# Proj matmuls two steps behind, staging five steps earlier, and the epilogue in one piece, in a fused attention and FFN kernel on eight cores

## The chip, the cores and the metric

The kernel runs on the 8 NeuronCores of one Trainium2 chip. The time is the device time of the slowest core in microseconds (us), the median of the runs given.

## The reference

The input x is 16 x 2048 tokens of 1024 features, in fp32. The reference is one pre-norm layer:

```python
x = x + attn(layernorm(x))
x = x + ffn(layernorm(x))
# attn: softmax(logits, axis=1), over a single head: every weight is 1,
#   so values are the sum of v over the sequence, times w_o: one row per batch
# ffn:
h = einsum('btd,hd->bth', x, absmean(W_fc))        # 1024 -> 4096, weights -1, 0, 1
h = gelu(h)
h = layernorm(h, ln_w, ln_b)                       # over the 4096
out = einsum('bth,dh->btd', h, absmean(W_proj))    # 4096 -> 1024, weights -1, 0, 1
```

`absmean` rounds each weight, divided by the mean of their absolute values, to -1, 0 or 1.

## The kernel before

Each core has two batches, 4096 tokens. A first stage of about 637 us reads x and the weights, works out the attention's row for each batch (ATT), and leaves the ternary weights in SBUF as bf16: `qf` for fc and `qp` for proj. The rest, the main stage, goes over 16 tiles of 256 tokens (two groups tg of 128), with 32 steps j in each, one per 128 hidden features. Activations in fp32 are split into three bf16 parts that add up to them, so each product is done three times.

Every engine has its own program in order, and the order is written out by hand; semaphores with constant counts tie them together. A step j of tile i is:

- TensorE, fc(j): 24 matmuls (3 parts x 8 slices of 128 input features) into `fc_ps[j % 2]`. It waits until gelu(j-2) has read that buffer (`ss_gelu`).
- ScalarE: gelu(j) from `fc_ps` into the single buffer `g`, after gps(j-1) is done with it (`sv_gdone`), and its square into `gsq`.
- VectorE, "gps(j)" in this text: it adds `g` to S1 and `gsq` to S2 (the sums for the layernorm; at j = 0 two copies), and splits `g` times ln_w into the three parts of a `gps` buffer, four operations; six in all. It waits with the first part until proj(j-2) has read the buffer (`st_projj`), and then counts `sv_gdone` up.
- TensorE, proj(j-1), right after fc(j): 12 matmuls into `proj_ps`, which gathers over the 32 steps. Proj 0 also waits for `sv_psr`, that is, until both halves of `proj_ps` of the tile before are evacuated.

Beside this, work for the tile i+1 is placed in the steps of tile i. VectorE does it after gps(j): x1 = x + ATT into one of four `x1s` buffers (`emit_x1_add`; it waits for the load of x, and with `sm_outs` for the store that was the last to read the buffer), its mean and variance (`emit_x1_bn`), the normalisation into `xs` (`emit_apply`), and 16 blocks that split `xs` into bf16 parts `l2t` (`emit_stage_block`, four operations each). TensorE transposes them into `trp_ps` (`emit_group_T`, 48 in all, two per step from j = 12; each waits for its block, `sv_stg`, and for ScalarE's evacuation of the one two before), and ScalarE copies them back to `l2t` (`emit_group_evac`). ScalarE also takes the square roots for the variances, for which it changes its activation table and changes it back.

At the end of a tile ("the boundary") TensorE does proj 31 and the transposes that are left. VectorE splits S1 and S2, TensorE sums them across partitions by four "S transposes" (L749), ScalarE evacuates these, VectorE makes mean and variance, and ScalarE two roots ("the roots", `ss_r3`). The epilogue of tile i-1 then lies in steps 0 to 5 of tile i, a piece after each gps: evacuation of `proj_ps[0]`, scaled and added to x1s; the same for `proj_ps[1]`; then for each group an operation with U and an addition of V, after which (`sv_y3`) POOL stores the group. Tile 15 has its epilogue in one piece at the end (`emit_epilogue`).

Of the kernel before, what the change touches and what calls it, by code (L numbers as in the profile page):

```python
# [64 lines left out]
def build_nc(nt=NTILE, do_b=True, do_main=True):  # L65
# [18 lines left out]
    with es:  # L84
# [27 lines left out]
        gps_t = sb("gps_t", (128, 1536), BF16)  # L112
        gps = [[gps_t[:, (k * 3 + s) * 256:(k * 3 + s) * 256 + 256] for s in range(3)]
               for k in range(2)]
# [101 lines left out]
        def emit_proj(tensor, i, jj):  # L216
            cglob = 32 * i + jj
            tensor.wait_ge(sv_gdone, cglob + 1)
            if jj == 0:
                if i >= 1:  # L220
                    tensor.wait_ge(sv_psr, 2 * i)
                else:
                    tensor.wait_ge(B_qp, 32)
                    tensor.wait_ge(B_uvbc, 2)
            last = None
            for tg in range(2):
                for s in range(3):
                    for hh in range(2):
                        last = tensor.matmul(out=proj_ps[tg][:, 512 * hh:512 * hh + 512],  # L229
                                      lhsT=gps[jj % 2][s][:, 128 * tg:128 * tg + 128],  # L230
                                      rhs=qp[jj][:, 512 * hh:512 * hh + 512],
                                      start=(jj == 0 and s == 0),
                                      stop=(jj == 31 and s == 2),
                                      skip_group_check=True)
            last.then_inc(st_projj, 1)

        def emit_epi_piece(vector, ii, piece):
            tg = piece // 3 if piece >= 2 else piece
            gr0, gr1 = 2 * ii, 2 * ii + 1
            if piece == 0:  # L240
                vector.wait_ge(ss_r3, ii + 1)
                vector.wait_ge(st_projj, 32 * (ii + 1))
                for tg_ in range(2):
                    vector.tensor_scalar(out=nmrc[tg_][:], in0=m3c[tg_][:],
                                         scalar1=r3c[tg_][:], scalar2=-2.0,
                                         op0=OP.mult, op1=OP.mult)
                vector.scalar_tensor_tensor(out=x1s[gr0 % 4][:], in0=proj_ps[0][:],
                                            scalar=r3c[0][:], in1=x1s[gr0 % 4][:],
                                            op0=OP.mult, op1=OP.add)
                vector.inc(sv_psr, 1)  # L250
            elif piece == 1:
                vector.scalar_tensor_tensor(out=x1s[gr1 % 4][:], in0=proj_ps[1][:],
                                            scalar=r3c[1][:], in1=x1s[gr1 % 4][:],
                                            op0=OP.mult, op1=OP.add)
                vector.inc(sv_psr, 1)
            elif piece in (2, 4):
                tg_ = 0 if piece == 2 else 1
                gr = 2 * ii + tg_
                vector.scalar_tensor_tensor(out=x1s[gr % 4][:], in0=U[:],
                                            scalar=nmrc[tg_][:], in1=x1s[gr % 4][:],  # L260
                                            op0=OP.mult, op1=OP.add)
            else:
                tg_ = 0 if piece == 3 else 1
                gr = 2 * ii + tg_
                vector.tensor_add(out=x1s[gr % 4][:], in0=x1s[gr % 4][:], in1=V[:])
                vector.inc(sv_y3, 1)
# [21 lines left out]
        def emit_x1_add(vector, ip1, tg):  # L288
            gr = 2 * ip1 + tg
            vector.wait_ge(sm_xs[gr % 2], 16 * (gr // 2 + 1))  # L290
            if gr >= 4:
                vector.wait_ge(sm_outs[gr % 4], 16 * (gr // 4))
            vector.tensor_add(out=x1s[gr % 4][:], in0=xs[gr % 2][:],
                              in1=ATT[gr // 16][:])

        def emit_x1_bn(vector, ip1, tg):
            gr = 2 * ip1 + tg
            vector.bn_stats(out=bnp[:, 0:6], in_=x1s[gr % 4][:, 0:512])
            vector.bn_stats(out=bnp[:, 6:12], in_=x1s[gr % 4][:, 512:1024])
            vector.bn_aggr(out=bno2[:, 2 * tg:2 * tg + 2], in_=bnp[:])  # L300
            vector.tensor_scalar_add(out=varc[:], in0=bno2[:, 2 * tg + 1:2 * tg + 2],
                                     scalar1=EPS)
            vector.reciprocal(out=rcc[tg][:], in_=varc[:])
            vector.inc(sv_stat, 1)

        def emit_x1_stats(vector, ip1, only_tg=None):
            for tg in ((0, 1) if only_tg is None else (only_tg,)):
                emit_x1_add(vector, ip1, tg)
                emit_x1_bn(vector, ip1, tg)
# [114 lines left out]
        def _(scalar):  # L424
# [72 lines left out]
            for i in range((nt + 1) if do_main else 0):  # L497
# [14 lines left out]
                if i <= nt - 1:  # L512
                    if i == 0:
                        for q in range(48):
                            emit_group_evac(scalar, 0, q)
                    scalar.preload_act_table(AF.Gelu)
                    for j in range(32):
                        cglob = 32 * i + j
                        scalar.wait_ge(st_fcj, cglob + 1)
                        if cglob >= 1:  # L520
                            scalar.wait_ge(sv_gdone, cglob)
                        scalar.activation(out=g[j % 2][:], in_=fc_ps[j % 2][:],
                                          func=AF.Gelu)
                        scalar.inc(ss_gelu, 1)
                        scalar.activation(out=gsq[j % 2][:], in_=g[j % 2][:], func=AF.Square)
                        scalar.inc(ss_gsq, 1)
                        if j in (8, 10) and i + 1 <= nt - 1:
                            tg = 0 if j == 8 else 1
                            scalar.preload_act_table(AF.Sqrt)
                            scalar.wait_ge(sv_stat, 2 * (i + 1) + tg + 1)  # L530
                            scalar.activation(out=r2c[tg][:], in_=rcc[tg][:],
                                              func=AF.Sqrt)
                            scalar.inc(ss_r2, 1)
                            scalar.preload_act_table(AF.Gelu)
                        if i + 1 <= nt - 1 and 13 <= j <= 31:
                            emit_group_evac(scalar, i + 1, 2 * (j - 13))
                            emit_group_evac(scalar, i + 1, 2 * (j - 13) + 1)
                    if i + 1 <= nt - 1:
                        for q in range(38, 48):
                            emit_group_evac(scalar, i + 1, q)  # L540
                    scalar.preload_act_table(AF.Sqrt)

        @block.tensor
        def _(tensor):
# [163 lines left out]
            for i in range(nt):  # L708
# [3 lines left out]
                for j in range(32):  # L712
# [16 lines left out]
                    if j >= 1:  # L729
                        emit_proj(tensor, i, j - 1)  # L730
                    if i + 1 <= nt - 1 and 12 <= j <= 31:
                        emit_group_T(tensor, i + 1, 2 * (j - 12))
                        emit_group_T(tensor, i + 1, 2 * (j - 12) + 1)
                emit_proj(tensor, i, 31)
                if i + 1 <= nt - 1:
                    for ql in range(40, 48):
# [18 lines left out]
        def _(vector):  # L755
# [160 lines left out]
            for i in range(nt):  # L916
                for j in range(32):
# [11 lines left out]
                    if cglob >= 2:  # L929
                        vector.wait_ge(st_projj, cglob - 1)  # L930
                    vector.tensor_scalar_mul(out=gps[j % 2][0][:], in0=g[j % 2][:],
# [3 lines left out]
                                                in1=gps[j % 2][0][:],  # L935
                                                op0=OP.mult, op1=OP.subtract)
                    vector.tensor_copy(out=gps[j % 2][1][:], in_=rrq1[:])
                    vector.tensor_tensor(out=gps[j % 2][2][:], in0=rrq1[:],
                                         in1=gps[j % 2][1][:], op=OP.subtract)
# [70 lines left out]
```

## Time and profile before

| | |
|---|---|
| median of 3 runs | 3812.06 us (3811.46 to 3812.66) |
| profiled execution, its own time | 3809.74 us |
| span of its slowest core, first to last instruction | 3808.2 us |
| spans of the eight cores | 3804.8 to 3808.2 us |
| mean granted TensorE clock, each core | 0.956 of full speed |
| TensorE busy | 2973.5 us |
| VectorE busy | 2238.7 us |
| ScalarE busy | 908.2 us |

The profile is one execution, seen on core 3, the slowest. Times in it are microseconds from the start of the span. PE is TensorE, DVE is VectorE, ACT is ScalarE; PEclk is the share of its full clock that TensorE was granted. Nearly all operations of VectorE and ScalarE go through one helper and carry its line, L51, so that they are told apart by the tiles that they write and read. Idle time of an engine that isn't the bottleneck costs nothing.

### The profile page before, as it was taken

The page shows a single profiled execution, that of the slowest core. Times are in us where ns is not written, and L with a number is a line of the kernel's source. Part 1 is how long each engine was busy: PE and PEld are TensorE (multiplying, and loading weights), DVE is VectorE, ACT ScalarE, POOL GpSimd, SP SyncE. Part 2 cuts the span into 40 slices and gives each one's busy share as a digit, 9 for nine tenths or more (in the row PEclk, how much of TensorE's full clock was granted, in tenths as well). Part 3 has the DMA queues.
Part 4 walks back from the last instruction along what each step waited for, and adds up shares of the span by engine and source line. Part 5 has one row for each costly group of instructions (what it writes and reads, how often), then busy time and mean ns, then how long its engine had stood idle before and what let it go on. Part 6 is the DMA issues. An engine that isn't in the chain of part 4 may idle for free.

```text
span 3808.2 us, 66893 instructions; the slowest of 8 cores (3804.8 to 3808.2 us)
## 1 busy us (share of the span) xinstructions
PE 2973.5 (78%) x22170; PEld 1989.3 (52%) x22170; DVE 2238.7 (59%) x5462; ACT 908.2 (24%) x2163; POOL 71.5 (2%) x148
## 2 busy tenths in 40 slices
PE   0002334989898998989898989898989898989896
PEld 0002232656565665656565656565656565656564
DVE  5667774656565555556555555555556565656554
ACT  1125202222222222222222222222222222222211
POOL 0000202000000000000000000000000000000000
PEclk9999999999999999999999999999999999999998
DMA  4439450000000000000000000000000000000000
GB/s 144 126 117 287 147 155 23 7 7 12 12 12 12 12 12 12 12 12 12 12 12 12 12 12 7 18 7 18 7 18 7 12 12 12 12 7 12 1 12 12
DMA packets 38403, 130.26 MB, mean 34 GB/s; under 512 B 7216, under 2 KB 7344, under 8 KB 38064
## 3 DMA queue, kind: packets, MB, share of 16 engines
q1 hardware_dynamic: 18864, 67.22, 5.9%
q10 hardware_dynamic: 9216, 33.56, 2.8%
q0 software_dynamic: 9984, 25.20, 1.9%
q8 instruction: 184, 3.01, 0.3%
q14 instruction: 155, 1.27, 0.1%
HBM read 109.15 MB, written 16.78 MB: 33 GB/s over the span
## 4 chain that ended last, share of the span: by engine, by line
PE 69%; DVE 12%; ACT 4%; DMA 4%; DVEq 4%; issue 4%; ACTq 1%; POOL 1%; SPq 0%; POOLq 0%
PE fc_ps L723 34%; PE proj_ps L229 33%; DVEq L50 4%; DVE cols L51 3%; DMA x1s<-wpT 2%; DVE gps_t L51 2%; DMA xs<-wfcT 1%; DVE rrq L51 1%; PE trp_ps L704 1%; DVE bnp L51 1%; ACTq L50 1%; ACT ATT L51 1%; DVE l2t_t L51 1%; DVE x1s L51 1%; ACT g L51 1%
## 5 line engine op out<-in xcount | busy, mean ns | idle before, releaser
L229 PE MATMUL proj_ps<-qp_t,gps_t 128*128 128x512 bf16 x6144 | 1442.3, 385 | 155.6 <-DVE x1s L51 139.1
L723 PE MATMUL fc_ps<-l2t_t,qf_t 128*128 128x256 bf16 x12288 | 1495.2, 281 | 0.7 <-ACT l2t_t L51 0.7
L723 PEld LDWEIGHTS fc_ps<-l2t_t,qf_t 128*128 128x128 bf16 x12288 | 1224.3, 101 | 211.5 <-issue 1.6
L229 PEld LDWEIGHTS proj_ps<-qp_t,gps_t 128*128 128x128 bf16 x6144 | 607.7, 99 | 803.0 <-issue 205.2
L51 DVE TENSOR_TENSOR S<-S,g 128x256 f32<-128x256 f32 x496 | 211.0, 425 | 859.9 <-ACT g L51 855.2
L51 ACT ACTIVATE g<-fc_ps 128x256 f32<-128x256 f32 x512 | 197.1, 385 | 2136.8 <-PE fc_ps L723 2095.8
L51 DVE SCALAR_TENSOR_TENSOR rrq<-g,lnw_c,gps_t 128x256 f32<-128x256 f32 x512 | 248.3, 485 | 41.0 <-issue 3.3
L51 ACT ACTIVATE l2t_t<-trp_ps 128x128 bf16<-128x128 f32 x768 | 213.2, 278 | 135.3 <-PE trp_ps L704 74.0
L51 DVE TENSOR_TENSOR gps_t<-rrq,gps_t 128x256 bf16<-128x256 f32 x512 | 217.6, 425 | 39.9 <-issue 2.6
L51 DVE TENSOR_TENSOR S<-S,gsq 128x256 f32<-128x256 f32 x496 | 210.9, 425 | 37.8 <-issue 1.5
L51 ACT ACTIVATE gsq<-g 128x256 f32<-128x256 f32 x512 | 213.3, 417 | 42.4 <-issue 1.4
L704 PE MATMUL trp_ps<-identb,l2t_t 128*128 128x128 bf16 x768 | 123.5, 221 | 118.8 <-DVE l2t_t L51 92.9
L557 PE MATMUL trp_ps<-identb,l2t_t 128*128 128x128 bf16 x48 | 6.6, 299 | 265.9 <-DVE l2t_t L51 264.7
L51 DVE TENSOR_SCALAR gps_t<-g,lnw_c 128x256 bf16<-128x256 f32 x512 | 180.8, 353 | 41.4 <-issue 1.7
L704 PEld LDWEIGHTS trp_ps<-identb,l2t_t 128*128 128x128 bf16 x768 | 75.1, 98 | 220.8 <-issue 149.5
L51 DVE CAST gps_t<-rrq 128x256 bf16<-128x256 f32 x512 | 150.6, 294 | 40.5 <-issue 3.4
L557 PEld LDWEIGHTS trp_ps<-identb,l2t_t 128*128 128x128 bf16 x48 | 4.0, 123 | 268.2 <-issue 267.6
L51 ACT ACTIVATE cols<-cols 128x1 f32<-128x1 f32 x96 | 22.4, 233 | 283.5 <-DVE cols L51 280.4
L51 DVE TENSOR_TENSOR l2t_t<-rrq,l2t_t 128x128 bf16<-128x128 f32 x256 | 74.7, 292 | 21.7 <-issue 3.2
L51 DVE TENSOR_TENSOR rrq<-xs,l2t_t 128x128 f32<-128x128 f32 x256 | 74.8, 292 | 19.1
L407 POOL DMA_DIRECT2D out<-x1s x32 | 17.1, 533 | 3177.6 <-DVE x1s L51 3177.6
L51 DVE CAST l2t_t<-xs 128x128 bf16<-128x128 f32 x256 | 58.2, 227 | 23.7 <-issue 0.5
(127 smaller groups left out, 1412.8 us busy)
## 6 DMA issues: line engine op xcount, KB each, us to landing
x1s<-wpT ACTq DMA_DIRECT2D x64, 512.0 KB, 4.9
xs<-x SPq DMA_DIRECT2D x64, 512.0 KB, 4.2
xs<-wfcT SPq DMA_DIRECT2D x64, 512.0 KB, 4.5
out<-x1s POOLq DMA_DIRECT2D x32, 512.0 KB, 3.0
x1s<-wvT POOLq DMA_DIRECT2D x8, 512.0 KB, 7.0
x1s<-woT POOLq DMA_DIRECT2D x8, 512.0 KB, 6.6
l2t_t<-gps_t POOLq DMA_DIRECT2D x96, 0.2 KB, 1.6
xs<-ident SPq DMA_DIRECT2D x1, 64.0 KB, 9.1
```

What stands on the lines that cost most here:

```text
L50: self._eng.drain()
L51: ins = attr(*a, **kw)
L229: last = tensor.matmul(out=proj_ps[tg][:, 512 * hh:512 * hh + 512], lhsT=gps[jj % 2][s][:, 128 * tg:128 * tg + 128], rhs=qp[jj][:, 512 * h ...
L407: gpsimd.dma_start(out=og[gr, :, :], in_=x1s[gr % 4][:]).then_inc(sm_outs[gr % 4], 16)
L557: last = tensor.matmul(out=trp_ps[g_ % 2][:], lhsT=lhs, rhs=identb[:], start=(s_ == 0), stop=(s_ == 2), skip_group_check=True)
L704: tensor.matmul(out=trp_ps[ql % 2][:], lhsT=lhs, rhs=identb[:], start=True, stop=True, skip_group_check=True).then_inc(st_tr, 1)
L723: last = tensor.matmul(out=fc_ps[j % 2][:], lhsT=qf[d][:, 128 * j:128 * j + 128], rhs=l2t[i % 2][s][d][:], start=(s == 0 and d == 0), stop ...
```

## The change

- `gps` has three buffers in place of two, and gps(j) waits for the third proj before it in place of the second. TensorE does proj(j-2) after fc(j) in place of proj(j-1); proj 30 and 31 follow after the last step.
- The epilogue of tile i-1 stands in one piece ahead of gps(0) of tile i.
- The statistics of tile i+1 are done at j = 0 (first group) and j = 2, in one piece each, in place of j = 6 to 9; the applies at j = 5 and 6 in place of 10 and 11; the blocks at j = 7 to 22 in place of 12 to 27.
- ScalarE takes both roots for them at j = 4, with one change of table and back, in place of j = 8 and 10 with one each. Transposes start at j = 10 in place of 12 and their evacuations at 11 in place of 13; after the last step 4 and 6 of them are left in place of 8 and 10.

```diff
-        gps_t = sb("gps_t", (128, 1536), BF16)
+        gps_t = sb("gps_t", (128, 2304), BF16)
...
-               for k in range(2)]
+               for k in range(3)]
...
-                                      lhsT=gps[jj % 2][s][:, 128 * tg:128 * tg + 128],
+                                      lhsT=gps[cglob % 3][s][:, 128 * tg:128 * tg + 128],
...
-                        if j in (8, 10) and i + 1 <= nt - 1:
-                            tg = 0 if j == 8 else 1
+                        if j == 4 and i + 1 <= nt - 1:
                             scalar.preload_act_table(AF.Sqrt)
-                            scalar.wait_ge(sv_stat, 2 * (i + 1) + tg + 1)
-                            scalar.activation(out=r2c[tg][:], in_=rcc[tg][:],
-                                              func=AF.Sqrt)
-                            scalar.inc(ss_r2, 1)
+                            for tg in range(2):
+                                scalar.wait_ge(sv_stat, 2 * (i + 1) + tg + 1)
+                                scalar.activation(out=r2c[tg][:], in_=rcc[tg][:],
+                                                  func=AF.Sqrt)
+                                scalar.inc(ss_r2, 1)
                             scalar.preload_act_table(AF.Gelu)
-                        if i + 1 <= nt - 1 and 13 <= j <= 31:
-                            emit_group_evac(scalar, i + 1, 2 * (j - 13))
-                            emit_group_evac(scalar, i + 1, 2 * (j - 13) + 1)
+                        if i + 1 <= nt - 1 and 11 <= j <= 31:
+                            emit_group_evac(scalar, i + 1, 2 * (j - 11))
+                            emit_group_evac(scalar, i + 1, 2 * (j - 11) + 1)
                     if i + 1 <= nt - 1:
-                        for q in range(38, 48):
+                        for q in range(42, 48):
...
-                    if j >= 1:
-                        emit_proj(tensor, i, j - 1)
-                    if i + 1 <= nt - 1 and 12 <= j <= 31:
-                        emit_group_T(tensor, i + 1, 2 * (j - 12))
-                        emit_group_T(tensor, i + 1, 2 * (j - 12) + 1)
+                    if j >= 2:
+                        emit_proj(tensor, i, j - 2)
+                    if i + 1 <= nt - 1 and 10 <= j <= 31:
+                        emit_group_T(tensor, i + 1, 2 * (j - 10))
+                        emit_group_T(tensor, i + 1, 2 * (j - 10) + 1)
+                emit_proj(tensor, i, 30)
                 emit_proj(tensor, i, 31)
                 if i + 1 <= nt - 1:
-                    for ql in range(40, 48):
+                    for ql in range(44, 48):
                         emit_group_T(tensor, i + 1, ql)
...
             for i in range(nt):
+                if i >= 1:
+                    emit_epilogue(vector, i - 1)
                 for j in range(32):
...
-                    if cglob >= 2:
-                        vector.wait_ge(st_projj, cglob - 1)
+                    if cglob >= 3:
+                        vector.wait_ge(st_projj, cglob - 2)
...
-                    if i >= 1 and j <= 5:
-                        emit_epi_piece(vector, i - 1, j)
                     if i + 1 <= nt - 1:
-                        if j == 6:
-                            emit_x1_add(vector, i + 1, 0)
-                        elif j == 7:
-                            emit_x1_bn(vector, i + 1, 0)
-                        elif j == 8:
-                            emit_x1_add(vector, i + 1, 1)
-                        elif j == 9:
-                            emit_x1_bn(vector, i + 1, 1)
-                        elif j == 10:
+                        if j == 0:
+                            emit_x1_stats(vector, i + 1, 0)
+                        elif j == 2:
+                            emit_x1_stats(vector, i + 1, 1)
+                        elif j == 5:
                             emit_apply(vector, i + 1, 0)
-                        elif j == 11:
+                        elif j == 6:
                             emit_apply(vector, i + 1, 1)
-                        elif 12 <= j <= 27:
-                            emit_stage_block(vector, i + 1, j - 12)
+                        elif 7 <= j <= 22:
+                            emit_stage_block(vector, i + 1, j - 7)
```

`emit_x1_stats` is the addition of `emit_x1_add` followed by the operations of `emit_x1_bn`.

## Rows read from the trace of the kernel before

**Rows 1.** The page: busy time, share of the span and instructions of each engine

```profile
PE 2973.5 (78%) x22170; PEld 1989.3 (52%) x22170; DVE 2238.7 (59%) x5462; ACT 908.2 (24%) x2163; POOL 71.5 (2%) x148
```

**Rows 2.** The chain that ended last, in order of time: start, us, what

```profile
841.80 4.29 PE proj_ps L229 x12
...
1830.53 4.86 PE proj_ps L229 x12
1835.38 2.62 PE fc_ps L723 x24
1838.00 2.59 PE proj_ps L229 x12
...
3612.30 4.85 PE proj_ps L229 x12
```

**Rows 3.** Timeline of TensorE at a boundary and at j = 12 to 15

```profile
1802.00 2.75 PE L229 MATMUL proj_ps<-qp_t,gps_t 128*128 128x512 bf16 x12
...
1814.13 7.07 PE L723 MATMUL fc_ps<-l2t_t,qf_t 128*128 128x256 bf16 x48
...
1887.32 2.78 PE L723 MATMUL fc_ps<-l2t_t,qf_t 128*128 128x256 bf16 x24
...
1912.26 0.28 PE L704 MATMUL trp_ps<-identb,l2t_t 128*128 128x128 bf16 x2
1912.37 2.78 PE L723 MATMUL fc_ps<-l2t_t,qf_t 128*128 128x256 bf16 x24
```

**Rows 4.** Waits from 1000 to 3600 us: us in total, times, longest

```profile
PE trp_ps L704 <- DVE l2t_t L51: 66.5, 26, 2.9
```

**Rows 5.** Stretches: us, busy time of each engine, granted clock (PEclk), DMA

```profile
1888.00:1910.00 22.00, 16.87 (x98) 10.89 (x96) 8.54 (x24) 2.34 (x7) 0.00 (x0) 0.84 0.00 1
...
3617.00:3768.00 151.00, 151.00 (x1045) 102.14 (x1044) 73.83 (x176) 23.25 (x58) 1.06 (x2) 1.00 0.02 8
```

**Rows 6.** Timeline of ScalarE at a boundary, and its table load at j = 8

```profile
1808.76 2.95 ACT L51 ACTIVATE l2t_t<-trp_ps 128x128 bf16<-128x128 f32 x8 [3.18 <-PE trp_ps L704]
...
1818.59 0.66 ACT L51 ACTIVATE cols<-cols 128x1 f32<-128x1 f32 x2 [4.00 <-DVE cols L51]
...
1820.62 0.38 ACT L51 ACTIVATE g<-fc_ps 128x256 f32<-128x256 f32 x1
...
1870.36 1.28 ACT L529 ACT_TABLE_LOAD   x1
```

**Rows 7.** Timeline of VectorE in the tile after that boundary

```profile
1821.16 0.29 DVE L51 COPY S<-g 128x256 f32<-128x256 f32 x1 [2.69 <-ACT g L51]
...
1838.74 0.43 DVE L51 TENSOR_TENSOR S<-S,g 128x256 f32<-128x256 f32 x1 [8.36 <-ACT g L51]
...
1841.09 0.42 DVE L51 TENSOR_TENSOR gps_t<-rrq,gps_t 128x256 bf16<-128x256 f32 x1
...
1862.45 1.23 DVE L51 TENSOR_TENSOR x1s<-xs,ATT 128x1024 f32<-128x1024 f32 x1
...
1867.83 1.46 DVE L51 BATCH_NORM_STATS2 bnp<-x1s 128x6 f32<-128x512 f32 x2
...
1870.13 0.42 DVE L51 TENSOR_TENSOR S<-S,g 128x256 f32<-128x256 f32 x1
...
1883.58 0.81 DVE L51 TENSOR_SCALAR xs<-x1s,cols 128x1024 f32<-128x1024 f32 x1
...
1894.68 0.29 DVE L51 TENSOR_TENSOR l2t_t<-rrq,l2t_t 128x128 bf16<-128x128 f32 x1
```

**Rows 8.** Timeline of the final epilogue, from its roots on

```profile
3784.27 0.66 ACT L51 ACTIVATE cols<-cols 128x1 f32<-128x1 f32 x2 [4.17 <-DVE cols L51]
...
3791.65 0.53 POOL L407 DMA_DIRECT2D out<-x1s  x1 [150.34 <-DVE x1s L51]
3792.55 1.23 DVE L51 TENSOR_TENSOR x1s<-x1s,V 128x1024 f32<-128x1024 f32 x1
```

**Rows 9.** The stores, from issue to landing, over the whole span

```profile
DMA to landing us min/median/max: 2.9/3.0/4.0
```

More of the change, by code:

```diff
@@ L235, in emit_proj @@
             last.then_inc(st_projj, 1)
[L237 to L266, printed above, removed]
         def emit_epilogue(vector, ii):
@@ L286, in emit_epilogue @@
                 vector.inc(sv_y3, 1)
[L288 to L304, printed above, removed]
         def emit_x1_stats(vector, ip1, only_tg=None):
             for tg in ((0, 1) if only_tg is None else (only_tg,)):
-                emit_x1_add(vector, ip1, tg)
-                emit_x1_bn(vector, ip1, tg)
+                gr = 2 * ip1 + tg
+                vector.wait_ge(sm_xs[gr % 2], 16 * (gr // 2 + 1))
+                if gr >= 4:
+                    vector.wait_ge(sm_outs[gr % 4], 16 * (gr // 4))
+                vector.tensor_add(out=x1s[gr % 4][:], in0=xs[gr % 2][:],
+                                  in1=ATT[gr // 16][:])
+                vector.bn_stats(out=bnp[:, 0:6], in_=x1s[gr % 4][:, 0:512])
+                vector.bn_stats(out=bnp[:, 6:12], in_=x1s[gr % 4][:, 512:1024])
+                vector.bn_aggr(out=bno2[:, 2 * tg:2 * tg + 2], in_=bnp[:])
+                vector.tensor_scalar_add(out=varc[:], in0=bno2[:, 2 * tg + 1:2 * tg + 2],
+                                         scalar1=EPS)
+                vector.reciprocal(out=rcc[tg][:], in_=varc[:])
+                vector.inc(sv_stat, 1)
         def emit_apply(vector, ip1, tg):
@@ L928, in _ @@
                         vector.tensor_add(out=S2[:], in0=S2[:], in1=gsq[j % 2][:])
-                    if cglob >= 2:
-                        vector.wait_ge(st_projj, cglob - 1)
-                    vector.tensor_scalar_mul(out=gps[j % 2][0][:], in0=g[j % 2][:],
+                    if cglob >= 3:
+                        vector.wait_ge(st_projj, cglob - 2)
+                    gsl = gps[cglob % 3]
+                    vector.tensor_scalar_mul(out=gsl[0][:], in0=g[j % 2][:],
                                              scalar1=lnw_c[:, j:j + 1])
@@ L934, in _ @@
                                                 scalar=lnw_c[:, j:j + 1],
-                                                in1=gps[j % 2][0][:],
+                                                in1=gsl[0][:],
                                                 op0=OP.mult, op1=OP.subtract)
-                    vector.tensor_copy(out=gps[j % 2][1][:], in_=rrq1[:])
-                    vector.tensor_tensor(out=gps[j % 2][2][:], in0=rrq1[:],
-                                         in1=gps[j % 2][1][:], op=OP.subtract)
+                    vector.tensor_copy(out=gsl[1][:], in_=rrq1[:])
+                    vector.tensor_tensor(out=gsl[2][:], in0=rrq1[:],
+                                         in1=gsl[1][:], op=OP.subtract)
                     vector.inc(sv_gdone, 1)
-                    if i >= 1 and j <= 5:
-                        emit_epi_piece(vector, i - 1, j)
                     if i + 1 <= nt - 1:
-                        if j == 6:
-                            emit_x1_add(vector, i + 1, 0)
-                        elif j == 7:
-                            emit_x1_bn(vector, i + 1, 0)
-                        elif j == 8:
-                            emit_x1_add(vector, i + 1, 1)
-                        elif j == 9:
-                            emit_x1_bn(vector, i + 1, 1)
-                        elif j == 10:
+                        if j == 0:
[3 more added lines that the diff above has]
+                        elif j == 5:
                             emit_apply(vector, i + 1, 0)
-                        elif j == 11:
+                        elif j == 6:
                             emit_apply(vector, i + 1, 1)
-                        elif 12 <= j <= 27:
-                            emit_stage_block(vector, i + 1, j - 12)
+                        elif 7 <= j <= 22:
+                            emit_stage_block(vector, i + 1, j - 7)
                 if i >= 1:
```

## The prediction

> **What bounds the kernel now.** I read the page first: TensorE is busy 78% of the span, VectorE 59%, ScalarE 24% [rows 1]. Then the chain in order of time: in the dense part of a tile TensorE alternates 2.62 us (24 fc matmuls) and 2.59 us (12 proj matmuls) with nothing between [rows 2]. One step is 5.21 us. A pair of transposes adds 0.11 us (1912.26 to 1912.37) [rows 3]. I call P the start of a tile's first proj group; in the middle of the run it is 1830.53. From the first P of a tile with a predecessor, 841.80, to the last, 3612.30, are 14 periods, 197.89 us each [rows 2]. As 32 steps of 5.21 us are only 166.7 us, each tile loses some 31 us, and TensorE's timeline shows two places.
>
> Place one is the tile boundary. Let F be the end of the last fc group, 1802.00, where proj 30 starts. Then come proj 31, the last transposes, the S transposes, and fc 0 and 1, which end at 1821.20 (1814.13 + 7.07) [rows 3]. From there TensorE stands 9.33 us until P: proj 0 waits for gps(0), the evacuation of both proj halves and the gps(1) between them, all VectorE's. F to P is 28.53 us.
>
> Place two is j = 12 and 13. TensorE asks for a block's transposes right after proj 11 (12), while VectorE makes that block only after gps(12) (13), which needs the fc group just finished. The chain of waits has 26 such waits over 13 tiles, 66.5 us [rows 4], and what follows each runs at a lowered clock: granted 0.84 in this stretch, where the dense part of the last tile has 1.00 [rows 5]; the levels are 1.2 and 2.4 GHz. From the start of fc 12 (1887.32) to that of fc 15 (1912.37) are 25.05 us, where three steps with transposes take 15.96 [rows 3]: 9.1 us lost per tile, in tiles 0 to 14.
>
> **The change, part by part.** (a) *Transposes from j = 10, blocks at j = 7 to 22.* Block 0 is made three steps before it is asked for; TensorE then uses 2/3 of a block per step and VectorE makes one, so the lead grows. The 9.1 us go if VectorE gets to j = 7 in time, which (d) works out. Two more steps with transposes lie before F: 0.2 us. After F, 4 transposes are left in place of 8.
>
> (b) *Proj two steps behind fc.* TensorE's work is the same in sum, its order isn't: at F proj 29, 30 and 31 are open, not 30 and 31, and fc 0, 1 and 2 can run before P, not 0 and 1. Fc 2 needs gelu(0), which ends at 1821.00 (1820.62 + 0.38) [rows 6], just as fc 1 ends. Between P and F are then 29 proj and 29 fc groups, not 30 and 30: 5.2 us less per tile, if F to P doesn't grow. The third buffer is what allows it: gps(3) waits for proj 0.
>
> (c) *F to P, the epilogue in one piece ahead of gps(0).* First, F to the roots. ScalarE's last transposed block ends at 1811.71 (1808.76 + 2.95) [rows 6]. With the change, proj 29, a pair, proj 30 and 31 take 7.88 us from F, to 1809.88; gps(31) was ready 3.5 us after F. The evacuations start 0.35 us later and are four, not eight; a pair more takes 0.77 us (2.95 = 3 x 0.77 + 0.64), so they end at 1811.64: no difference. Table load, S transposes and the reductions follow as now, up to the end of the two roots at 1819.25 (1818.59 + 0.66) [rows 6]. Second, roots to P. The final epilogue has the code that now stands ahead of every gps(0); from the end of its roots (3784.27 + 0.66) to that of its last addition (3792.55 + 1.23) are 8.85 us [rows 8], and it doesn't wait for gelu(0). Then gps(0): a usual gps takes 2.77 us (1838.74 to 1841.51), and its first two operations are copies here, 0.29 in place of 0.43 us [rows 7]: 2.49, and 0.09 ahead of it. With 0.15 us for the signal to TensorE, P is 11.6 us after the roots, against 11.28 now (1819.25 to 1830.53). So F to P becomes 28.8 us, with fc 2 inside the former wait, of which about 7 us are left.
>
> (d) *VectorE after P,* where the gain could be lost. Let 0 be the end of gps(0). From one gps to the next are 0.15 (signal), 0.39 (gelu), 0.15 (signal) and 2.77: 3.45 us. The statistics of a block between them make it 0.1 + 1.23 (addition) + 0.1 + 2.30 (bn_stats to the next operation, 1867.83 to 1870.13) + 2.77: 6.5 us [rows 7]. So gps(1) ends at 6.5, (2) at 9.95, (3) at 16.45, (4) at 19.9. At j = 4 ScalarE, free from 17.6, spends 3.2 us on two table loads of 1.28 and two roots (0.66) [rows 6], so gelu(5) starts at 20.8 and gps(5) ends at 24.1. Each apply adds at most 1.3 us (0.81 and a small operation) and a block 1.5 (four of at most 0.29 with gaps) [rows 7]: gps(6) at 28.3, gps(7) at 32.5, block 0 at 34. TensorE: proj 0 from 0.15 at the low clock, 4.67 us to fc 3 (1830.53 to 1835.2), so that it wants proj 1 at 7.4, proj 2 at 12.7, proj 3 at 17.9, proj 4 at 23.1, proj 5 at 28.3, block 0 at 46.5. All are ready, proj 1 by 0.8 us, proj 3 by 1.3 us. If proj 0 ran in 2.59 us, proj 1 would be waited for, and 0.8 us would be gained.
>
> (e) *The store.* The first statistics of tile i, at gps(0), now wait for the store of tile i-1 from the same x1s buffer. POOL issues it 6.7 us after the roots (3784.93 to 3791.65) [rows 8]; landing takes 3.0, at most 4.0 us [rows 9]: 9.7 to 10.7 us, and VectorE asks at 11.5. Hidden, by 0.8 to 1.8 us; a store 5 us later would cost about 3.5 us a tile. Its instruction on POOL delays nothing, as POOL has no other work here. The load of x was issued a tile earlier. The larger gps_t and one table switch for two cost nothing.
>
> **The sum.** P to F: 4.67 + 28 x 2.59 + 29 x 2.62 + 21 x 0.11 = 155.5 us; with 28.8 a period of 184.3 for 197.9: 13.6 us less, 14 times, 190. Tile 0 saves its 9.1 and one proj group, minus 0.2: 11.5. The last tile has no place two and saves 5.2 - 0.3 = 4.9. After it the S transposes wait for three proj groups rather than for the splitting of S: 0.5 lost, at most 0.8. In all 206 us. From the profiled execution's 3809.74 (span 3808.2) this leaves 3603.7; that execution lies 2.3 us under the median of the runs, 3812.06. I predict 3605.
>
> All dense stretches that I read have the full clock, 151 us of the last tile at 1.00 with TensorE busy throughout, on every core [rows 5]. The Trainium skill (TensorE: Matmul & The Clock Gate, Part 1) states a peak-current limit that takes a die to 13/16 of the clock once three of its cores run dense matmuls; it speaks against a denser kernel, but this trace, with eight cores dense, doesn't show it.
>
> **Rivals.** 1. *VectorE starves TensorE after P.* Epilogue and statistics are packed into the first steps, and the margin is 0.8 us. If gelu, the store or an operation comes a few us later than the rows say, all of (b) can be given back: 5.2 x 15 = 78 us, 3683. For it: the thin margin. Against: each duration has a row, and it takes some 6 us more per tile.
>
> 2. *The clock stays high through the shorter wait before P.* 0.8 x 15 = 12 us less: 3593. Against: waits of 2.6 us (66.5 / 26) already lower it [rows 4, 5].
>
> 3. *Slower: the full clock is no longer granted in the dense part.* That part is 16 x 155 = 2480 us. At 0.84, the lowest mean that a busy stretch shows [rows 5], it would take 472 us more: 4077. The gain is gone once its mean is below 2480 / (2480 + 206) = 0.92. Against: 1.00 wherever TensorE is busy throughout. By the 13/16 of the skill's page it would be 572 us more, 4177.
>
> 4. *Place two moves to j = 10 and 11.* That takes VectorE 12 us late (46.5 less 34). Only (b) would remain: 3605 + 15 x 9.1 = 3741.
>
> **How the numbers follow.** The forecast 77%, rival 1 in whole or part 10%, rival 2 7%, rivals 3 and 4 3% each. The likeliest case's own range is 3590 to 3620, as proj 0 after its wait took between 4.29 and 4.86 us [rows 2] and F to P rests on differences of 0.3 us, each times 15. Down past rival 2 and up to nearly half of rival 1 it is 3582 to 3640. Slower comes from rival 3 and from a store late beyond any row; within 0.2%, about what a measurement here can tell from no change, lies no named case: 0.95 faster, 0.01, 0.04 slower.
>
> **What would show it.** Right: no wait for l2t_t at j = 10 to 13; a period of 184 us; 72 fc matmuls and then some 7 us of idle time before P, ended by gps_t, not x1s; proj 0 above 4 us; granted clock 1.00 from there to F. Wrong: idle time before proj 1 or 3 ended by gps_t, VectorE waiting ahead of the first x1s addition, or a clock below 1.00 in the dense part.

## The result and the profile after

The changed kernel takes 3607.73 us, the median of 8 executions (3604.92 to 3615.34), against 3812.06 us before on the same chips: a ratio of 0.9461, 95% interval 0.945 to 0.9472. The forecast was 3605, and 206 us of gain; measured are 204. Each core had a mean granted clock of 0.975 in the profiled execution, where it was 0.956. In some executions, of the kernel before too, the cores of a die show a lower clock and the time is longer; the times and differences here leave these out (of the runs below two of four in e5, two of five in e7, and one each in e4, e6 and e8).

The page of the profiled execution, seen on core 5: its span, the busy times, and the group of proj matmuls with what ended its idle time.

```profile
span 3606.0 us, 66862 instructions; the slowest of 8 cores (3595.9 to 3606.0 us)
...
PE 2900.8 (80%) x22170; PEld 1959.1 (54%) x22170; DVE 2238.4 (62%) x5462; ACT 869.7 (24%) x2133; POOL 71.6 (2%) x148
...
L229 PE MATMUL proj_ps<-qp_t,gps_t 128*128 128x512 bf16 x6144 | 1435.2, 385 | 106.5 <-DVE gps_t L51 106.5
```

VectorE is busy for 2238.4 us, as long as before [rows 1]; its work was moved, not cut. TensorE's busy time fell by 73 us with the same 22170 matmuls: that is matmuls which no longer run at the low clock. The other 130 us of the span's 202 are idle time that is gone.

The chain in order of time gives the last P, and the timeline of TensorE the first ones, the boundary in the middle and the steps after it (answering to [rows 2, 3]).

```profile
3415.16 4.50 PE proj_ps L229 x12
```

```profile
832.65 5.28 PE L229 MATMUL proj_ps<-qp_t,gps_t 128*128 128x512 bf16 x12 [7.05 <-DVE gps_t L51]
...
1729.60 5.34 PE L229 MATMUL proj_ps<-qp_t,gps_t 128*128 128x512 bf16 x24
1734.78 0.27 PE L666 MATMUL trp_ps<-identb,l2t_t 128*128 128x128 bf16 x2
...
1738.93 9.84 PE L685 MATMUL fc_ps<-l2t_t,qf_t 128*128 128x256 bf16 x72
1756.14 4.58 PE L229 MATMUL proj_ps<-qp_t,gps_t 128*128 128x512 bf16 x12 [7.38 <-DVE gps_t L51]
1760.55 2.78 PE L685 MATMUL fc_ps<-l2t_t,qf_t 128*128 128x256 bf16 x24
1763.17 2.75 PE L229 MATMUL proj_ps<-qp_t,gps_t 128*128 128x512 bf16 x12
```

There are 72 fc matmuls ahead of P, not 48, and proj 30 and 31 run as one block of 24. The wait before P is 6.75 to 7.46 us, and what ends it is gps_t, where it was x1s. From 832.65 to 3415.16 are 14 periods of 184.47 us, for 197.89 before and 184.3 in the forecast.

The waits from 1000 to 3400 us, the same view as [rows 4]: TensorE's largest wait is that before P, 13 times, and transposes wait for ScalarE alone; the 26 waits for l2t_t are not there any more.

```profile
PE proj_ps L229 <- DVE gps_t L51: 92.0, 13, 7.4
...
PE trp_ps L666 <- ACT l2t_t L51: 6.6, 13, 0.5
```

A stretch that holds j = 10 to 13 and most of a tile, the same view as [rows 5]: 150 us busy of 150, clock 1.00.

```profile
1761.00:1911.00 150.00, 150.00 (x1069) 102.57 (x1067) 92.79 (x251) 37.32 (x102) 0.00 (x0) 1.00 0.03 8
```

VectorE in the first steps of the tile (answering to [rows 7]): the end of the epilogue, gps(0), the statistics right behind it, and the starts of what follows.

```profile
1752.05 1.23 DVE L51 TENSOR_TENSOR x1s<-x1s,V 128x1024 f32<-128x1024 f32 x1
1753.36 0.29 DVE L51 COPY S<-g 128x256 f32<-128x256 f32 x1
...
1755.46 0.42 DVE L51 TENSOR_TENSOR gps_t<-rrq,gps_t 128x256 bf16<-128x256 f32 x1
1755.97 1.23 DVE L51 TENSOR_TENSOR x1s<-xs,ATT 128x1024 f32<-128x1024 f32 x1
...
1761.93 0.42 DVE L51 TENSOR_TENSOR gps_t<-rrq,gps_t 128x256 bf16<-128x256 f32 x1
...
1787.53 0.42 DVE L51 TENSOR_TENSOR gps_t<-rrq,gps_t 128x256 bf16<-128x256 f32 x1
...
1789.01 0.29 DVE L51 TENSOR_TENSOR l2t_t<-rrq,l2t_t 128x128 bf16<-128x128 f32 x1
```

The statistics start 0.09 us after gps(0) ends (1755.88), without a wait: the store had landed. Gps(1) ends at 1762.35, gps(7) at 1787.95 and block 0 at 1789.30, that is 6.5, 32.1 and 33.4 us after gps(0). The forecast had 6.5, 32.5 and 34.

### The profile page after: what moved, and what is told of

Its sections match the earlier page's. It is cut to its first block, busy times and chain, and to the rows that moved or that the text cites. A ratio compares the mean times of both kernels' runs of the same rounds, so it can differ in the third digit from the quotient of the medians.

```text
span 3606.0 us, 66862 instructions; the slowest of 8 cores (3595.9 to 3606.0 us)
## 1 busy us (share of the span) xinstructions
PE 2900.8 (80%) x22170; PEld 1959.1 (54%) x22170; DVE 2238.4 (62%) x5462; ACT 869.7 (24%) x2133; POOL 71.6 (2%) x148
## 4 chain that ended last, share of the span: by engine, by line
PE 73%; DVE 11%; DMA 5%; ACT 4%; DVEq 3%; issue 3%; ACTq 1%; POOL 1%; SPq 0%; POOLq 0%
PE proj_ps L229 38%; PE fc_ps L685 34%; DVE cols L51 3%; DVEq L50 3%; DVE x1s L51 3%; DMA x1s<-wpT 3%; DMA xs<-wfcT 2%; DVE bnp L51 1%; PE trp_ps L666 1%; ACT ATT L51 1%; ACT qf_t L51 1%; ACT qp_t L51 1%; POOL l2t_t L362 1%; ACTq L50 1%; DVE qf_t L51 1%
## 5 line engine op out<-in xcount | busy, mean ns | idle before, releaser
L685 PE MATMUL fc_ps<-l2t_t,qf_t 128*128 128x256 bf16 x12288 | 1445.3, 275 | 5.8 <-ACT g L51 5.1
L685 PEld LDWEIGHTS fc_ps<-l2t_t,qf_t 128*128 128x128 bf16 x12288 | 1199.0, 99 | 185.4 <-issue 10.7
L519 PE MATMUL trp_ps<-identb,l2t_t 128*128 128x128 bf16 x48 | 6.6, 299 | 266.2 <-DVE l2t_t L51 264.9
L666 PE MATMUL trp_ps<-identb,l2t_t 128*128 128x128 bf16 x768 | 114.0, 222 | 31.2 <-DVE l2t_t L51 16.1
L51 DVE TENSOR_REDUCE cols<-S 128x1 f32<-128x128 f32 x64 | 18.3, 286 | 89.4 <-ACT S L51 85.5
```

Of the source, the lines that this page charges most:

```text
L51: ins = attr(*a, **kw)
L519: last = tensor.matmul(out=trp_ps[g_ % 2][:], lhsT=lhs, rhs=identb[:], start=(s_ == 0), stop=(s_ == 2), skip_group_check=True)
L666: tensor.matmul(out=trp_ps[ql % 2][:], lhsT=lhs, rhs=identb[:], start=True, stop=True, skip_group_check=True).then_inc(st_tr, 1)
L685: last = tensor.matmul(out=fc_ps[j % 2][:], lhsT=qf[d][:, 128 * j:128 * j + 128], rhs=l2t[i % 2][s][d][:], start=(s == 0 and d == 0), stop ...
```

## The experiments

Eight more kernels were run. Every ratio is against the kernel before on the same chip. The first four take the change apart, the last four test its margins and what is left. The diffs are cut to the main lines of each edit; the words below each diff name what goes with them (the steps of ScalarE's evacuations, the third buffer, in e5 and e8 also work moved to other steps). F is the end of fc 31 and P the start of proj 0, as in the prediction.

**e1: before, transposes one step later.**

```diff
-                    if i + 1 <= nt - 1 and 12 <= j <= 31:
-                        emit_group_T(tensor, i + 1, 2 * (j - 12))
-                        emit_group_T(tensor, i + 1, 2 * (j - 12) + 1)
+                    if i + 1 <= nt - 1 and 13 <= j <= 31:
+                        emit_group_T(tensor, i + 1, 2 * (j - 13))
+                        emit_group_T(tensor, i + 1, 2 * (j - 13) + 1)
```

> The kernel before, with only the transposes one step later (from j = 13, evacuations from 14, two more left after the last step); blocks, epilogue pieces and proj order stay. Theory: place two is purely that TensorE asks for a block in the step in which VectorE makes it; one step later each block is ready, so 9.1 us a tile go, 15 x 9.1 = 136, and one more pair after the last step costs 0.77 us x 15 = 12: 3812 - 136 + 12 = 3688 (3680 to 3700). Rival (the stall only moves to where VectorE is behind, or the lowered clock there has another cause): no less than 3780. In the trace, by the theory: no wait of a transpose for l2t_t at j = 12 to 14, and the clock at 1.00 there.

Measured: 3689.57 us, ratio 0.9663 (0.962 to 0.9706); the theory said 3688. At j = 13 the pair goes without a wait and the fc group behind it takes its usual time:

```profile
1659.40 2.75 PE L229 MATMUL proj_ps<-qp_t,gps_t 128*128 128x512 bf16 x12
1661.99 0.28 PE L704 MATMUL trp_ps<-identb,l2t_t 128*128 128x128 bf16 x2
1662.10 2.78 PE L723 MATMUL fc_ps<-l2t_t,qf_t 128*128 128x256 bf16 x24
```

So 123 of the 205 us could be had by shifting the transposes one step, with nothing else touched. The rival, a stall that only moves, has fallen.

**e2: before, with proj two steps behind and three buffers alone.**

```diff
-                    if j >= 1:
-                        emit_proj(tensor, i, j - 1)
+                    if j >= 2:
+                        emit_proj(tensor, i, j - 2)
...
+                emit_proj(tensor, i, 30)
                 emit_proj(tensor, i, 31)
...
-                    if cglob >= 2:
-                        vector.wait_ge(st_projj, cglob - 1)
+                    if cglob >= 3:
+                        vector.wait_ge(st_projj, cglob - 2)
```

> The kernel before, with only part (b): three gps buffers and proj(j-2) after fc(j); staging from j = 12 and the epilogue in pieces stay. Theory: one proj and one fc group less between P and F, 5.2 us a tile; but now F to the roots holds three proj groups and eight transposes, 7.88 + 0.35 + 2.95 = 11.2 us in place of 9.7, 1.5 us more; place two stays at 9.1 us. Net 3.7 x 15 = 55: 3757 (3745 to 3770). Rival (the third buffer also lets TensorE through place two, since proj no longer waits there): about 3620 to 3680. Rival (the order of proj gives nothing by itself): 3812.

Measured: 3756.03 us, ratio 0.9839 (0.9795 to 0.9883), 56 us less than before and well clear of the noise; the theory said 3757. Place two is as before, proj 10 in place of proj 11 being what lies ahead of the wait:

```profile
1671.13 2.75 PE L229 MATMUL proj_ps<-qp_t,gps_t 128*128 128x512 bf16 x12
1676.41 0.50 PE L704 MATMUL trp_ps<-identb,l2t_t 128*128 128x128 bf16 x2 [2.53 <-DVE l2t_t L51]
1676.77 4.18 PE L723 MATMUL fc_ps<-l2t_t,qf_t 128*128 128x256 bf16 x24
```

**e3: the changed kernel with proj one step behind.**

```diff
-                    if j >= 2:
-                        emit_proj(tensor, i, j - 2)
+                    if j >= 1:
+                        emit_proj(tensor, i, j - 1)
...
-                emit_proj(tensor, i, 30)
```

> The changed kernel with only part (b) taken back: proj(j-1) after fc(j), gps still in three buffers. Theory: 5.2 us a tile more between P and F, but F to the last evacuation becomes shorter: proj 31 starts 3.7 us after F, ends at 6.3, and with four transposes left the evacuations end at 8.0 in place of 9.7, 1.6 us less. Net 3.6 x 15 = 54: 3608 + 54 = 3662 (3650 to 3675). TensorE's wait before P about 9.7 us in place of 7.4. Rival (VectorE's packed work after P, not the order, is what limits the start of a tile): with proj 1 wanted earlier there would be waits before proj 1 and 3 ended by gps_t, and 3690 or more.

Measured: 3668.95 us, ratio 0.9615 (0.9571 to 0.9659): 61 us over the changed kernel, where 54 were expected. The period is as forecast, (3469.25 - 834.46) / 14 = 188.2, 3.7 more than 184.47. What the 54 lacked is mostly the last tile, which has a proj and an fc group more behind its P and gets nothing back from a shorter tail: it takes 5.9 us more from P to the end. The wait before P is 9.8 to 11.8 us, and behind it none of the first proj groups waits (two do in tile 0, 1.1 and 1.2 us), so VectorE's packed work isn't what limits.

```profile
1587.53 4.40 PE L229 MATMUL proj_ps<-qp_t,gps_t 128*128 128x512 bf16 x12 [9.96 <-DVE gps_t L51]
1591.76 2.78 PE L685 MATMUL fc_ps<-l2t_t,qf_t 128*128 128x256 bf16 x24
1594.38 2.75 PE L229 MATMUL proj_ps<-qp_t,gps_t 128*128 128x512 bf16 x12
```

With e2 and the result this makes a square: proj order alone -56, all the rest alone -143, together -204 us. The parts add up, within 5 us.

**e4: the changed kernel with transposes from j = 12.**

```diff
-                    if i + 1 <= nt - 1 and 10 <= j <= 31:
-                        emit_group_T(tensor, i + 1, 2 * (j - 10))
-                        emit_group_T(tensor, i + 1, 2 * (j - 10) + 1)
+                    if i + 1 <= nt - 1 and 12 <= j <= 31:
+                        emit_group_T(tensor, i + 1, 2 * (j - 12))
+                        emit_group_T(tensor, i + 1, 2 * (j - 12) + 1)
```

> The changed kernel with transposes from j = 12 and evacuations from 13 again, eight and ten left after the last step; blocks still from j = 7, so none is waited for. It prices the tail after F alone. Theory: two more pairs of transposes with their evacuations stand after proj 31, on the path to the roots: 2 x 0.77 x 15 = 23 us, less 2 x 0.11 x 15 = 3 that leave the steps: 3608 + 20 = 3628 (3620 to 3635). Rival (the tail is hidden beside VectorE's split of S): 3605 to 3610.

Measured: 3634.13 us, ratio 0.9519 (0.9466 to 0.9571); its executions lie between 3629.7 and 3637.4, apart from the profiled one, 3673.8, of which more below. It is 22 to 30 us over the changed kernel, and 20 were expected. TensorE asks for the first block at j = 12 here, as before, but VectorE makes it at j = 7, and no transpose in the tiles waits for l2t_t. The timeline of ScalarE shows the longer tail: it evacuates four pairs after proj 31, until 1747.21, where the changed kernel needs two.

```profile
1744.17 0.64 ACT L51 ACTIVATE l2t_t<-trp_ps 128x128 bf16<-128x128 f32 x2 [4.65 <-PE trp_ps L666]
1745.03 2.18 ACT L51 ACTIVATE l2t_t<-trp_ps 128x128 bf16<-128x128 f32 x6 [0.21 <-PE trp_ps L666]
1747.22 1.28 ACT L503 ACT_TABLE_LOAD   x1
```

So the tail is on the path, and going from j = 13 (e1) to j = 10 is worth something beyond the stall.

**e5: the changed kernel, evacuations first.**

```diff
-                if i >= 1:
-                    emit_epilogue(vector, i - 1)
+                if i >= 1:
+                    emit_evac(vector, i - 1)      # nmrc, and proj_ps[0], [1] into x1s
...
+                    if i >= 1:
+                        if j == 0:
+                            emit_u(vector, i - 1, 0)
+                        elif j == 1:
+                            emit_v(vector, i - 1, 0)
+                        elif j == 2:
+                            emit_u(vector, i - 1, 1)
+                            emit_v(vector, i - 1, 1)
```

> The changed kernel with the epilogue taken apart again, but otherwise than before: ahead of gps(0) only what proj 0 waits for, the two evacuations; the operations with U and V after gps(0), (1) and (2), two for the second group there; statistics after gps(3) and (5), ScalarE's roots at j = 7, applies after gps(8) and (9), blocks from j = 10, transposes from j = 11 (six left). Theory: from the roots to P are 0.2 + 0.5 + 2.7 + 2.5 + gaps = 6.2 us in place of 11.8, one more pair after the last step costs 0.8: 4.8 us a tile. The wait before P shrinks from 7.4 to 1.8 us; if the clock then stays up, proj 0 takes 2.6 in place of 4.5 us: up to 6.7 a tile. 3608 - 72 to 3608 - 100: 3508 to 3536. Rival (VectorE bounds the first steps, so an earlier P is given back at proj 1 to 6): 3580 or more, with waits for gps_t there.

Measured: 3508.9 and 3509.7 us, against 3811.62 before. That is 98 us under the changed kernel, at the far end of 72 to 100. The wait before P is 1.7 us in most tiles, 1.0 to 1.9 in the others but one, and proj 0 then runs at full speed. In one of the 15 tiles the wait was 2.09 us, and proj 0 took 4.44.

```profile
1704.09 9.84 PE L709 MATMUL fc_ps<-l2t_t,qf_t 128*128 128x256 bf16 x72
1715.81 2.75 PE L229 MATMUL proj_ps<-qp_t,gps_t 128*128 128x512 bf16 x12 [1.88 <-DVE gps_t L51]
...
2072.08 4.44 PE L229 MATMUL proj_ps<-qp_t,gps_t 128*128 128x512 bf16 x12 [2.09 <-DVE gps_t L51]
```

VectorE as the bound, the rival, has fallen: the periods are 177.6 to 178.2 us, and no proj group behind P waits for it. The one tile with a slow proj 0 took 179.32 us.

**e6: the changed kernel with four more bn_stats.**

```diff
-                vector.bn_stats(out=bnp[:, 0:6], in_=x1s[gr % 4][:, 0:512])
+                for _ in range(5 if (tg == 0 and ip1 >= 1) else 1):
+                    vector.bn_stats(out=bnp[:, 0:6], in_=x1s[gr % 4][:, 0:512])
```

> The changed kernel, the first bn_stats of the first group of each tile repeated four times (same result), so that 4 x 0.77 = 3.1 us of VectorE's work are added after gps(0). It measures the margin of step (d). Theory: in the changed kernel's trace gps(1) ends 1762.35 and proj 1 starts 1763.17, so 0.67 us are to spare after the signal; 2.4 us a tile are lost, 15 times: 3608 + 36 = 3644 (3638 to 3650), with a wait before proj 1 ended by gps_t. Rival (the margin is elastic, a slow proj 0 or the third buffer takes it up): 3608 to 3615. Rival (a late VectorE stays late up to the transposes and the loss grows): over 3660.

Measured: 3656.1 us, ratio 0.9592 (0.9573 to 0.9611): 48 us more and not 36; the period is 187.75 us, 3.3 more than 184.47. The margin was right and the cost of going past it wasn't. Proj 1 starts 9.44 us after P in both tiles below (the changed kernel: 7.03, at 1763.17), which is the 2.4 us of the forecast. But if proj 0 was quick to come up to full clock, TensorE waits 2.64 us for proj 1, and then runs that one at the low clock too, 4.44 us. It does so in seven of the 14 tiles, whose periods are 188.4 to 189.1 us; in the other seven, with waits of 1.2 to 1.6 us before proj 1, they are 186.5 to 187.2.

```profile
1022.05 4.17 PE L229 MATMUL proj_ps<-qp_t,gps_t 128*128 128x512 bf16 x12 [7.20 <-DVE gps_t L51]
1026.06 2.78 PE L686 MATMUL fc_ps<-l2t_t,qf_t 128*128 128x256 bf16 x24
1031.49 4.44 PE L229 MATMUL proj_ps<-qp_t,gps_t 128*128 128x512 bf16 x12 [2.64 <-DVE gps_t L51]
...
1210.44 5.28 PE L229 MATMUL proj_ps<-qp_t,gps_t 128*128 128x512 bf16 x12 [7.03 <-DVE gps_t L51]
1215.51 3.08 PE L686 MATMUL fc_ps<-l2t_t,qf_t 128*128 128x256 bf16 x24
1219.88 2.75 PE L229 MATMUL proj_ps<-qp_t,gps_t 128*128 128x512 bf16 x12 [1.29 <-DVE gps_t L51]
```

**e7: the changed kernel with transposes from j = 8.**

```diff
-                    if i + 1 <= nt - 1 and 10 <= j <= 31:
-                        emit_group_T(tensor, i + 1, 2 * (j - 10))
-                        emit_group_T(tensor, i + 1, 2 * (j - 10) + 1)
+                    if i + 1 <= nt - 1 and 8 <= j <= 31:
+                        emit_group_T(tensor, i + 1, 2 * (j - 8))
+                        emit_group_T(tensor, i + 1, 2 * (j - 8) + 1)
...
-                if i + 1 <= nt - 1:
-                    for ql in range(44, 48):
-                        emit_group_T(tensor, i + 1, ql)
```

> The changed kernel with transposes from j = 8 and evacuations from 9, so that none is left after the last step. Block 0 is ready at 1789.3 in the changed kernel's trace, and TensorE asks for it after proj 6 of j = 8, at 1791.8 there. Theory: the tail after F was on the path, and with it gone the table load lies beside proj 30 and 31: the S transposes start right after proj 31 (F + 7.9) and are copied at F + 8.3 in place of F + 11.0; 2.7 us a tile less, 0.2 for the two more steps with pairs: 2.5 x 15 = 37: 3571 (3563 to 3580). Rival (the place-two stall comes back at j = 8 or 9, since VectorE is only 2.5 us ahead): 3600 or more, with waits for l2t_t. Rival (VectorE's split of S, ready at F + 7.2, or something behind it takes over): 3590 to 3605.

Measured: 3572.2 us, ratio 0.9376 (0.9357 to 0.9394), with executions from 3569.5 to 3578.4; 3571 was expected, and no transpose waits for l2t_t in the tiles. S transposes follow proj 31 at once, and the table load, at 1723.03 in this trace, lies beside it. A wait took the place of part of the gain, without a cost: fc 2 is now ready 1.65 us before gelu(0) is, but the wait before P is longer still.

```profile
1722.13 5.34 PE L229 MATMUL proj_ps<-qp_t,gps_t 128*128 128x512 bf16 x24
1727.31 0.50 PE L709 MATMUL trp_ps<-identb,Ss_t 128*128 128x128 bf16 x6
...
1728.79 5.40 PE L685 MATMUL fc_ps<-l2t_t,qf_t 128*128 128x256 bf16 x48
1735.85 2.78 PE L685 MATMUL fc_ps<-l2t_t,qf_t 128*128 128x256 bf16 x24 [1.65 <-ACT g L51]
1746.01 4.05 PE L229 MATMUL proj_ps<-qp_t,gps_t 128*128 128x512 bf16 x12 [7.38 <-DVE gps_t L51]
```

**e8: both, with VectorE's work spread.**

```diff
-                if i + 1 <= nt - 1:
-                    for ql in range(44, 48):
-                        emit_group_T(tensor, i + 1, ql)
+                if i + 1 <= nt - 1:
+                    for ql in range(46, 48):
+                        emit_group_T(tensor, i + 1, ql)
+                emit_proj(tensor, i, 31)
...
+                        if j == 2:
+                            emit_x1_add(vector, i + 1, 0)
+                        elif j == 3:
+                            emit_x1_bn(vector, i + 1, 0)
+                        elif j == 4:
+                            emit_x1_add(vector, i + 1, 1)
+                        elif j == 5:
+                            emit_x1_bn(vector, i + 1, 1)
+                        elif j == 6:
+                            emit_apply(vector, i + 1, 0)
+                            emit_apply(vector, i + 1, 1)
```

> Both of the former together, with VectorE's added work spread by what each step can bear: evacuations ahead of gps(0); U and V operations after gps(0), (1), (1), (2); addition and statistics singly after gps(2) to (5); roots at j = 6; both applies after gps(6); blocks from j = 7; transposes from j = 9, the one pair left after the last step put between proj 30 and 31. Theory: F to the roots 2.7 us shorter, the roots to P 5.6 us shorter, proj 0 up to 1.9 us shorter if the clock stays up, 0.1 for one more step with a pair: 8.2 to 10.1 us a tile, 3608 - 123 to 3608 - 152: 3456 to 3485. Rival (VectorE bounds the first steps): 3500 to 3560, with waits for gps_t before proj 1 to 7.

Measured: 3476.44 us, ratio 0.912 (0.9102 to 0.9138), faster than both kernels, 131 us under the changed one. The period is (3283.54 - 822.40) / 14 = 175.8, 8.7 less. Proj 0 takes 2.75 us, and the granted clock of each core is 0.995 or 0.996. No proj group behind P waits for gps_t, so the rival has fallen in its own terms. But VectorE isn't quite ahead of the steps: in tiles 1 to 14 the second pair of transposes (j = 10) waits 0.3 to 1.2 us for ScalarE's evacuation, a loss that the expectation didn't have. In the tile below, where it is largest, ScalarE was late because its gelu(10) had waited for gps(9).

```profile
1570.30 0.57 PE L697 MATMUL trp_ps<-identb,l2t_t 128*128 128x128 bf16 x2 [1.16 <-ACT l2t_t L51]
...
1685.25 2.75 PE L229 MATMUL proj_ps<-qp_t,gps_t 128*128 128x512 bf16 x12
1687.84 0.50 PE L743 MATMUL trp_ps<-identb,Ss_t 128*128 128x128 bf16 x6
...
1689.32 5.40 PE L716 MATMUL fc_ps<-l2t_t,qf_t 128*128 128x256 bf16 x48
1696.38 2.78 PE L716 MATMUL fc_ps<-l2t_t,qf_t 128*128 128x256 bf16 x24 [1.66 <-ACT g L51]
1701.04 2.75 PE L229 MATMUL proj_ps<-qp_t,gps_t 128*128 128x512 bf16 x12 [1.88 <-DVE gps_t L51]
```

ScalarE, with the gelu that came late (1568.92) and the evacuation behind it:

```profile
1568.92 0.38 ACT L51 ACTIVATE g<-fc_ps 128x256 f32<-128x256 f32 x1 [3.90 <-DVE gps_t L51]
...
1569.88 0.64 ACT L51 ACTIVATE l2t_t<-trp_ps 128x128 bf16<-128x128 f32 x2
```

## Why the prediction was right

(a) *Place two.* Gone, with its waits and its low clock. E1 shows that the cause was the one named, the block asked for in the step that makes it, and prices it with one more pair in the tail at 123 us (124 expected). E4 shows it from the other side: asking at j = 12 costs no stall once the block is made at j = 7.

(b) *Proj two behind.* The order is what gives the gain: e2 has it alone, -56 us against 55 worked out beforehand, and e3 takes it back, +61.

(c) *F to P.* F is 1726.9 in the trace after (proj 30 and 31 start at 1729.60, 2.70 us later). The roots end 17.2 us after F, as they did before, so the forecast that three proj groups and four transposes fit where two and eight were holds. From the roots (1744.09) to P are 12.05 us in this tile, 0.43 of it a pause of VectorE inside the epilogue; in tiles with the shorter wait of 7.03 it is 11.7. Forecast was 11.6. F to P is 28.9 to 29.3 us (29.6 in the first tile with a predecessor) for a forecast 28.8. One row was misread, without effect: gps(31) was ready 3.67 us after F and not 3.5. No run has the epilogue in one piece alone; e5, which puts only the two evacuations ahead of gps(0) and moves the rest and the statistics back, wins 98 us over the changed kernel, the most of any single part that was tried (e7, the tail after F, wins 36).

(d) *VectorE after P.* All times of the forecast's schedule were met within 0.6 us, and the margin of 0.8 us before proj 1 was measured as 0.67 and confirmed by e6. Rival 1 was a real danger: 3.1 us more of work cost 3.3 us per tile, of the 5.2 that it could take at most by the prediction. What the prediction didn't have is the way in which it costs: not only the lateness, 2.4 us, but in half of the tiles a second group at the low clock.

(e) *The store.* POOL issued it at 1751.15 and a store takes 2.9 us to land in this trace; the addition of the statistics came at 1755.97 and didn't wait. This margin, 1.9 us, was not tried by an experiment.

The sum: tile 0, from its first fc to the next P, became 11.7 us shorter (forecast 11.5), 14 periods 13.4 each (13.6), the last tile with the end 5.1 (4.4). That is 204.7 (forecast 206). In the profiled execution the stage ahead of the tiles took 2.5 us longer, which the change doesn't touch, so that the span fell by 202.2. So the total is right term by term, and not by errors that cancel.

Rival 2, the clock staying up, didn't happen in the changed kernel (proj 0 takes 4.45 to 5.28 us), but it does in e5 and e8, where the wait is 1.7 us. Its price of 0.8 us, worked out from VectorE's lateness before proj 1, was not tested by any run. In e5, where VectorE doesn't bind, the tile with the slow proj 0 took 1.7 us more than most others (179.32 against 177.63). Rival 3 didn't happen: the mean clock was 0.974 to 0.976 on every core in the 8 executions. Rival 4 didn't happen, and e7 shows that even j = 8 isn't too early.

## What to carry to other kernels

In engines that run hand-ordered programs, look for the step in which a consumer asks for what its producer makes in that same step; a lead of one step took away 9 us per tile here, and its low clock with it. Of the work between two tiles, put first only what the next tile's first matmul waits for, and spread the rest over the steps by what each can bear: a running sum of VectorE's added work against TensorE's time per step, as in (d), told in advance where TensorE would wait for VectorE (e6) and where not (e5, e7). It must hold ScalarE's steps too: e8's wait, which came to TensorE through ScalarE, was not foreseen. Work that TensorE can do before the wait at a boundary is worth its full time, as long as what comes after is not needed sooner than it is ready.

## What the runs showed of the hardware

A short wait can cost more than itself. In the kernel before, the fc group behind each wait for a block (2.5 to 2.9 us) took 4.1 to 4.5 us for 2.8; in e2 it took 3.9 to 4.5, but for the first such wait (2.52 us), after which it took 2.78. Over all cores of the kept traces, the proj and fc groups that are recorded whole and start right behind a wait of 1.0 to 3.0 us show three ranges: after less than 1.95 us all 489 ran at full speed; after 1.95 to 2.09 us 21 of 63 ran slow, 4.05 to 4.45 us, and the others didn't (2.09 us did the one in e5, 4.44 us, and the other in e8, 2.75 us); after 2.19 to 3.00 us all 54 ran slow, 4.1 to 4.4 us, all of them in e6. What decides in the middle range stays open.

The Trainium skill (TensorE: Matmul & The Clock Gate, Part 1) tells that idle time takes the clock to half, 1.2 GHz; the trace of the changed kernel agrees, with a granted clock of 0.50 over the first P group, which took 5.28 us for 2.75:

```profile
832.65:837.72 5.07, 5.07 (x12) 1.78 (x13) 4.38 (x10) 0.68 (x2) 0.00 (x0) 0.50 0.01 3
```

A group of 4.1 to 4.9 us is slow for its first part only: of the P group at 1756.14 (4.58 us), the first 2.36 us have 0.50, the first 4.36 us 0.57 on the mean.

In the profiled execution of e4 the clock was lowered, in some stretches and on some cores at a time, while TensorE was busy throughout. These are stretches of core 2 and of core 1 in the same die, each with the columns of [rows 5]. Core 1's mean of 0.97 in the second holds a tile boundary; its 150 us before, busy throughout, have 1.00.

```profile
3460.00:3600.00 140.00, 139.03 (x790) 86.92 (x800) 53.00 (x133) 18.09 (x46) 0.00 (x0) 0.81 0.00 1
```

```profile
3460.00:3600.00 140.00, 132.41 (x908) 89.43 (x906) 71.45 (x174) 22.72 (x55) 1.06 (x2) 0.97 0.02 9
```

Core 1 itself was lowered earlier:

```profile
660.00:840.00 180.00, 180.00 (x1053) 112.67 (x1051) 91.59 (x248) 36.18 (x98) 0.00 (x0) 0.81 0.02 7
```

Cut into stretches of 30 us, the eight cores fall into four pairs that were lowered together: cores 0 and 1 from 660 to 840 us, 6 and 7 in stretches from 660 to 960, 4 and 5 in stretches from 3340 to the end, 2 and 3 from 3450 to the end; elsewhere their stretches away from the boundaries have 1.00. An fc group takes 3.15 us at 0.81 for 2.62. By 180 x (1 - 0.81), 180 us at this clock cost about 34 us (an estimate), most of the 40 us by which this execution is longer than the other ones of e4. So rival 3's mechanism exists on this chip, but it came for part of an execution, and for one pair of a die while the other had the full clock. What sets it off stays open; no run here was made to tell. The Trainium skill (TensorE: Matmul & The Clock Gate, Part 1) has the level, 13/16, but tells of it as lasting and of the whole die, which this trace doesn't bear out.
